# A hold on GpSimd's gathers in a four-layer graph network: at most two in flight, signalled by parity

## The reference, cut to what matters

```python
h = maximum(layernorm(x), 0)
x = x + L0(h, edge_weight)      # messages x[src] * weight, summed over dst
h = maximum(layernorm(x), 0)
x = x + L1(h, edge_attr_2)      # 4 x 4 hat functions times x[dst] @ W, summed over src
h = maximum(layernorm(x), 0)
x = x + L2(h, edge_attr_8)      # edge-made weights, both directions
h = maximum(layernorm(x), 0)
x = x + L3(h, edge_attr_8)      # tensor products, silu, then an update of each node
```

## Time and profile before

| | us |
|---|---|
| median of 3 runs (4017.7 to 4024.07) | 4020.64 |
| span of the profiled execution | 4874.8 |
| of it GpSimd busy | 2760.8 (57%) |
| of it VectorE busy | 2768.7 (57%) |
| of it TensorE busy, matmuls | 2006.0 (41%) |
| of it ScalarE busy | 1193.8 (24%) |

### The profile page before, as it was taken

The page is one execution under the profiler, slowest core; times in us unless marked ns, Lnnn a source line. Parts: engine busy times, 40 slices in busy tenths (PEclk is TensorE's granted clock), DMA queues, the critical chain, the costliest instruction groups (busy, mean ns, idle before and its releaser), DMA issues.

```text
span 4874.8 us, 28541 instructions
## 1 busy us (share of the span) xinstructions
PE 2006.0 (41%) x7574; PEld 1399.7 (29%) x7574; DVE 2768.7 (57%) x4103; ACT 1193.8 (24%) x2921; POOL 2760.8 (57%) x2767
## 2 busy tenths in 40 slices
PE   1200124434310002444443066666623554546998
PEld 0000013323200002333332044444412443434444
DVE  9108425545412403555557766677684565656988
ACT  0000113223221102333333233333322222221111
POOL 4777755655677775555551255555505555553786
PEclk6555556667655556777776577777766776778999
DMA  5000212322301101222225122222342222223010
GB/s 157 9 8 15 66 51 98 99 80 98 78 25 50 57 22 37 82 87 86 86 78 118 65 71 88 80 87 82 88 136 62 82 87 77 83 81 88 31 34 27
DMA packets 192773, 345.55 MB, mean 71 GB/s; under 512 B 81018, under 2 KB 159466, under 8 KB 164067
## 3 DMA queue, kind: packets, MB, share of 16 engines
q1 hardware_dynamic: 103104, 287.51, 16.0%
q0 software_dynamic: 81344, 21.38, 6.2%
q10 hardware_dynamic: 8164, 34.85, 1.9%
HBM read 66.26 MB, written 277.24 MB: 70 GB/s over the span
## 4 chain that ended last, share of the span: by engine, by line
DVE 26%; another core or an unknown queue 23%; issue 19%; PE 16%; POOL 11%; ACT 2%; SPq 2%; ACTq 1%; DMA 1%; DVEq 0%; POOLq 0%
POOL edges_by_dst L489 8%; DVE natS L1238 7%; PE psK L586 5%; PE psX L733 4%; PE psK L582 4%; DVE work L1238 3%; DVE work L1218 3%; DVE natD L1238 2%; POOL natD L531 1%; PE psX L644 1%; DVE psX L1291 1%; DVE natD L1283 1%; SPq L436 1%; SPq L437 1%
## 5 line engine op out<-in xcount | busy, mean ns | idle before, releaser
L507 POOL DMA_INDIRECT rows<-table,rec x1760 | 1679.9, 955 | 1661.6 <-issue 513.3
L586 PE MATMUL psK<-work 128*128 128x256 f32 x2640 | 832.8, 478 | 698.5 <-issue 389.1
L586 PEld LDWEIGHTS psK<-work 128*128 128x128 f32 x2640 | 629.7, 248 | 878.5 <-issue 585.1
L1238 DVE SCALAR_TENSOR_TENSOR natS<-natS,keep,psK 128x256 f32<-128x256 f32 x1069 | 513.6, 480 | 336.9 <-remote 246.8
L859 ACT ACTIVATE work<-iota,rec 128x128 f32<-128x128 f32 x1760 | 539.3, 393 | 638.7 <-remote 341.2
L1218 DVE TENSOR_TENSOR work<-at_hi,psX 128x2048 f32<-128x2048 f32 x220 | 502.4, 2284 | 4.3 <-ACT psX L904 0.4
L489 POOL DMA_INDIRECT edges_by_dst<-natD,pos x391 | 388.9, 995 | 171.0 <-issue 128.3
L489 POOL DMA_INDIRECT edges_by_src<-natS,pos x391 | 394.3, 1008 | 127.4 <-issue 127.4
L733 PE MATMUL psX<-natD,work 128*128 128x512 f32 x784 | 349.6, 598 | 17.6 <-DMA work<-scan_by_column 9.5
L582 PE MATMUL psK<-work 128*128 128x128 f32 x1760 | 303.0, 352 | 126.1 <-DVE work L1218 80.1
L582 PEld LDWEIGHTS psK<-work 128*128 128x128 f32 x1760 | 292.5, 264 | 190.2 <-DVE work L1218 127.9
(11 more groups left out here) (157 smaller groups left out, 2404.5 us busy)
## 6 DMA issues: line engine op xcount, KB each, us to landing
scan<-natS SPq DMA_DIRECT2D x110, 1024.0 KB
scan<-natD SPq DMA_DIRECT2D x28, 1024.0 KB
scan_by_column<-work SPq DMA_DIRECT2D x28, 1024.0 KB
rows<-table,rec POOLq DMA_INDIRECT x1760
scan<-work SPq DMA_DIRECT2D x27, 1024.0 KB
scan_by_column<-natS SPq DMA_DIRECT2D x27, 1024.0 KB
table<-h ACTq DMA_DIRECT2D x28, 896.0 KB, 3.6
work<-scan SPq DMA_DIRECT2D x126, 128.0 KB, 2.1
```

The costliest lines, as they stand in the source:

```text
L507: pool.indirect_dma_start(out=rows[k][:, u * D:(u + 1) * D], out_offset=None, in_=table.ap(), in_offset=bass.IndirectOffsetOnAxis(ap=rec[k ...
L586: k = nc.tensor.matmul(psK[:, o:o + BW], lo, spread[par][:, o:o + BW], start=True, stop=True)
L1238: V.scalar_tensor_tensor(acc[par][:, t * BW:(t + 1) * BW], was, keep[s][:, q * G + t:q * G + t + 1], psK[:, t * BW:(t + 1) * BW], ALU.mult ...
```

## The change

GpSimd waits ahead of each gather, except the first two of the run. Gather u of a group waits until the gather two places before it on the queue has landed, over the borders of groups and layers. For this the gathers signal on two semaphores, one for even and one for odd tiles, in place of one for each of the four slots of the ring. Whoever waits for a group's rows waits on both.

```diff
--- before.py
+++ after.py
@@ -242,7 +242,7 @@
                  ("taken", "outer", "hats", "hatsraw")]
         ed = [{n: sem(f"e{l}_{n}") for n in names if n not in lacks[l]} for l in range(4)]
 
-        gath = [sem(f"gath{k}") for k in range(RING)]
+        gath = [sem(f"gath_of_parity{p}") for p in range(2)]
         rec_in = [sem(f"rec{k}") for k in range(RING)]
         run_out = [sem(f"out{p}") for p in range(2)]
 
@@ -290,8 +290,13 @@
 
             return 16 * (past(l, g % RING, RING) + turns(g, RING))
 
-        def gathered(l, g):
-            return 16 * G * (past(l, g % RING, RING) + turns(g, RING))
+        def gathered(l, g, done=G):
+
+            return 16 * ((l * GROUPS + g) * (G // 2) + done // 2)
+
+        def wait_rows(eng, l, g):
+            eng.wait_ge(gath[0], gathered(l, g))
+            eng.wait_ge(gath[1], gathered(l, g))
 
         def kept_runs(l, g):
 
@@ -504,11 +509,13 @@
 
                         pool.wait_ge(used, g - RING + 1)
                     for u in range(G):
+                        if l or g or u >= 2:
+                            pool.wait_ge(gath[u % 2], gathered(l, g, u - u % 2))
                         pool.indirect_dma_start(
                             out=rows[k][:, u * D:(u + 1) * D], out_offset=None, in_=table.ap(),
                             in_offset=bass.IndirectOffsetOnAxis(
                                 ap=rec[k][:, u * F + f:u * F + f + 1].bitcast(i32), axis=0))\
-                            .then_inc(gath[k], 16)
+                            .then_inc(gath[u % 2], 16)
                 if l == 0:
                     place(1)
 
@@ -665,7 +672,7 @@
                     if l == 1:
                         outer_products(g)
                     elif l:
-                        pe.wait_ge(gath[k], gathered(l, g))
+                        wait_rows(pe, l, g)
                         if l == 2:
                             root_rows(g)
                         nc.tensor.transpose(psT[:, (k % 2) * P:(k % 2 + 1) * P], rows[k][:, :], ident[:, :])\
@@ -1246,7 +1253,7 @@
 
                     k = g % RING
                     dve.wait_ge(e["hats"], g + 1)
-                    dve.wait_ge(gath[k], gathered(l, g))
+                    wait_rows(dve, l, g)
                     V.tensor_tensor(outer.rearrange("p (u b i) -> p u b i", b=4, i=D),
                                     v3(rows[k][:, :])[:, :, None, :].to_broadcast([P, G, 4, D]),
                                     hat_of(k, 1)[:, :, :, None].to_broadcast([P, G, 4, D]), ALU.mult)\
```

## The result

The changed kernel takes 4664.15 us (median), the kernel before in the same runs 4019.7 us: ratio 1.161, 95% interval 1.160 to 1.163, so 644 us slower. Forecast were 4518 us and a range of 4150 to 4700.

The account below looks back on a forecast made before the run. GpSimd's issue of gathers was taken to set the loops' pace; 0.4 us quiet plus 2.0 us beside writes a group, less slack in layers 2 and 3, gave 497 us on 4020.6: 4518 us, range 4150 to 4700.

Parts of the forecast that it names:

- The bound: Message loops: in timed runs GpSimd's gather issue, 1.25 us each, paces layers 0 and 1, nearly layers 2 and 3.
- the rebuilt time: Whole kernel before: profiled span 4874.8 us less 857 us of stalls in the four layers gives 4018 us.
- Part 1, the hold: GpSimd, 1758 gathers: each waits for the one two before; a met wait costs nothing; place(1) passes layer 0's delay on.
- Part 2, the quiet release: Gathers away from writes: release takes 2.61 us where 2.50 are free, 0.4 us a group (bounds 0 and 0.8).
- Part 3, beside a write: Gathers during each group's 1 MB scan write: fewer land, so fewer are issued; 2.0 us a write (bounds 0 and 3.2).
- Part 4, two semaphores: Readers VectorE and TensorE: 220 more waits, hidden by the gathers' pace, cost 0 (11 us at most if not hidden).
- The slack: Layers 2 and 3: their loops run slower than GpSimd needs, so 26 and 5 us of the added time are absorbed.
- The sum: All four layers: 2.4 us a group, giving 132, 132, 106 and 127 us, total 497 us.
- Hidden: Rival, GpSimd: the hold falls into waits that the timed runs have too; 4021 us, chance 0.10.
- A packet at a time: Rival, scan writes: a gather yields only one packet per turn, 1.0 us a group, 189 us, 4210 us; chance 0.17.
- Faster: Rival, TensorE's stalls: gathers in flight cause them, so two in flight would free it; 3960 us, chance 0.08.
- What the profile should show: Changed profile: gather steps 1.3 us quiet, 2 to 4 in writes; new waits about 530 us; record waits near 400 or less.

Follow-up runs that it names:

- e1: Kernel before, no hold, but even and odd tiles' gathers signal on separate semaphores and readers wait on both: 4016.67 us against 4016.53, ratio 1.000.
- e8: Kernel before with a ninth gather a group into a spare tile nobody reads: 4256.38 us against 4022.98, ratio 1.058.
- e2: Changed kernel with the hold reaching back eight gathers instead of two, readers waiting on eight semaphores: 4016.08 us, ratio 1.000 to the kernel before.
- e9: Kernel before with split semaphores and the hold in layer 0 alone: 4186.76 us against 4020.66.
- e7: Changed kernel with scan writes and the loads of their sums cut to 16 of 128 partitions (128 KB for 1 MB): 4375.73 us.
- e6: Kernel before with scan writes and the loads of their sums cut to 16 of 128 partitions: 4014.86 us, ratio 0.998 to the kernel before.
- e12: Kernel before with each record load followed by a second one into a spare tile: 4019.3 us, ratio 1.000.

## Why the prediction was right, and where it was short

- *The bound.* Right: e1 has 549, 553, 583, 548 us for the gathers, and e8 shows the pace from the other side. That the rebuilt time came within 3 us of the median (4018 for 4020.6) was in part luck. Against e1, the start up to the first gather was taken 17 us too long (567 for 550) and layer 0 with place(1) 20 too long (1075 for 1055); layers 1, 2 and 3 were taken 10, 22 and 3 too short (560, 586 and 565 for 570, 608 and 568). The errors cancel.
- *Part 1, the hold.* Right: a wait that is met is free (e2), and one that binds costs by the landing, with 0.50 us on top at first gathers. The gather at 2014.30 showed no such cost because its waits were met. What stood behind it on GpSimd's queue, place(1), carried layer 0's share to the end (e9: 166 of 165).
- *Part 2, the quiet release.* The step that was mis-sized: 0.4 us a group forecast, 0.9 measured away from writes. The release itself was read well: 2.61 forecast, 2.35 + 0.26 measured. Working from its mean was wrong in kind: a late release costs, an early one gives nothing back, so the spread counts by its late side alone. The small lateness I had in mind (steps under 0.35 us late) is worth 60 / 220 = 0.3 us. The larger ones had no term. Two fifths of them are at a group's first gather, mostly by its later start, which the three releases of the earlier trace rows couldn't show, as other engines wait there. Another two fifths are gathers that land late with no write beside them, for a reason that is open.
- *Part 3, beside a write.* 2.0 forecast, 2.3 measured. The size from the packets that moved in a write was good. Going to 2.0 from between 1.4 and 2.0 was right; its reason, that the last one held waits out its own release too, fits the start at 2065.04 but was not tested. Some 0.2 of the 2.3 are late starts of first gathers and stands that fell beside a write.
- *Part 4, two semaphores.* Right: 0 (e1).
- *The slack.* 26 + 5 us forecast for layers 2 and 3, 34 + 0 measured in their gathers, and a further 21 in the lags of layers 1 to 3. By the prediction's own measure, first gather to last spread, layer 2 had 47 and not 26 to give, layer 1 had 10 and not 0.
- The sum: 220 x 2.4 - 31 = 497 forecast; 220 x 3.2 = 707, less some 60 of slack and lag, is the 644 measured. It is inside the range, near its upper end.
- *The rivals.* Hidden: out, it hung on the 847 us of waits for records, which the timed runs don't have. A packet at a time: 1.0 us a group, out by a factor of three. The rival took a turn to be one packet of the profile, which is 0.3 us; in the trace shown at e7 even the first packet of a gather is 1.0 us late, and a late gather's last one, in the median, 1.7. The Trainium skill (DMA: Bandwidth & Descriptors, "Queues, rings and completion order") has turns of a whole packet of typically 9 to 17 descriptors and does not say that this is one of the profile's, so the rival's price is not the skill's. How a DMA engine takes turns between the two queues no run here settles. The same section also says that a semaphore's increment lands only after the earlier writes of its DMA engine, from any queue. The trace leaves little room for that rule: of the 1.9 us by which late gathers land later, 1.7 lie ahead of their last data packet. Faster: out; no hold, at any depth, beat the kernel before.
- *What the profile should show.* Steps of about 1.3 us when quiet and 2 to 4 in a write, and new waits of 530 us (617 came): there. The waits for records fell from 847 to 4, but that tells little of the hold, as they are 49 without it (e1). From layer 0's first gather to layer 1's are 1220 us, 31 less than in the profile of the kernel before, whose stalls are gone, and 165 more than in e1.

## What to carry to other kernels

Before pricing a wait, find who sets the pace in the timed runs; where a profile is longer than they are, rebuild the time from its rows with the doubtful waits taken out, and see whether the median comes out. An engine that issues transfers every t us and must see the n-th before it land needs n x t well above the slowest release, not the mean one: here 2.5, 3.75 and 5.0 us of allowance cost 644, 187 and 21 us for a quiet release of 2.6. Price such a wait from the late side of the spread, from what else moves on the DMA engines meanwhile, and from how far behind the landing the next start comes (here 0.26 us, and 0.76 where a wait instruction of its own stands ahead).

## What was not expected of the hardware

- The profiled execution of the kernel before was 854 us over the timed ones, with long waits behind TensorE's semaphores; e1, e2, e6 and e12, which issue their gathers at the same pace, were profiled without such stalls (spans 4016.0, 4012.2, 4008.6 and 4021.9 us). So it seems to be that one execution and not the kernel, of which there is no second profile. What caused it isn't known.
- An eighth of a write's bytes keeps the gathers waiting for nearly half as long: 1.0 us a group beside 128 KB, 2.3 beside 1 MB (e7), and the write itself takes 2.6 us for 4.0.
- With the hold the mean granted clock of TensorE is lower, 0.698 against 0.735 in e1 (one in flight: 0.634). Its matmuls are busy for 44% of the span there and 48% in e1; what ties the clock to that, no run here shows.
- With the hold GpSimd stands some 2 us longer at one gather in 112. In e1, without it, the same gathers start after 0.30 us like all others.
